# Layer norms of a gated cross-attention stack: the scaling moved from the vector engine to the scalar engine

## What is computed

```
def _layernorm(x, axis=-1, eps=1e-05):
    m = jnp.mean(x, axis=axis, keepdims=True)
    v = jnp.var(x, axis=axis, keepdims=True)
    return (x - m) / jnp.sqrt(v + eps)
...
    x = x + jnp.tanh(g_xattn[0]) * _L0_xattn_ref(_layernorm(x, axis=-1), ctx_1024, ctx_1024, L0_xattn_random_features)
    x = x + jnp.tanh(g_ffn[0]) * _L0_ffn_ref(_layernorm(x, axis=-1), ...)
...
    x = x + jnp.tanh(g_ffn[3]) * _L3_ffn_ref(_layernorm(x, axis=-1), ...)
```

## Time and profile before

| | us |
|---|---|
| median of 3 runs | 2255.64 (2252.45 to 2267.68) |
| profiled execution, its own time | 2266.98 |
| its span | 2265.2 |
| TensorE busy | 1978.6 (87%) |
| VectorE busy | 1956.1 (86%) |
| ScalarE busy | 1472.5 (65%) |
| GpSimd busy | 949.1 (42%) |

### The profile page before, as it was taken

One profiled execution on the slowest core, in us unless ns is written; L12 is line 12 of the kernel. 1 busy time (PEld: TensorE's weight loads), 2 busy tenths in 40 slices (PEclk: granted clock), 3 DMA queues, 4 the chain that ended last, 5 costly groups with the idle time before them and its releaser, 6 DMA issues. The chain is left out here.

```text
span 2265.2 us, 41466 instructions
## 1 busy us (share of the span) xinstructions
PE 1978.6 (87%) x12569; PEld 1576.8 (70%) x12569; DVE 1956.1 (86%) x7828; ACT 1472.5 (65%) x3637; POOL 949.1 (42%) x1374
## 2 busy tenths in 40 slices
PE   5877788888998899988998899998998899788677
PEld 4555567766886679766886579766886579667456
DVE  1289797998989999998989999998999999795982
ACT  3545467787677767787577767787577767477431
POOL 3232322555165534555165534555255543332441
PEclk9888898999999999999999999999999999898788
DMA  4000101001100101001100101001100001001000
GB/s 191 1 8 1 36 1 57 1 1 36 44 16 1 36 6 54 2 2 36 43 18 1 36 1 57 4 1 36 39 22 1 27 3 57 31 1 57 1 3 3
DMA packets 29503, 55.03 MB, mean 24 GB/s; under 512 B 2914, under 2 KB 10082, under 8 KB 28642
## 3 DMA queue, kind: packets, MB, share of 16 engines
q1 hardware_dynamic: 29282, 52.37, 7.1%
HBM read 51.31 MB, written 1.05 MB: 23 GB/s over the span
## 5 line engine op out<-in xcount | busy, mean ns | idle before, releaser
L265 DVE MATCH_REPLACE8 top_work<-top_eight,top_work 128x256 f32<-128x256 f32 x1664 | 667.9, 409 | 0.0
L267 DVE MAX8 top_eight<-top_work 128x8 f32<-128x256 f32 x1664 | 617.2, 412 | 0.0
L305 POOL TENSOR_TENSOR top_p<-top_p,top_rest 128x512 f32<-128x512 f32 x192 | 244.2, 1272 | 155.5 <-ACT top_rest L298 154.3
L851 PE MATMUL bank<-workP 128*128 128x256 f32 x1024 | 278.4, 396 | 22.7 <-ACT att_pP L991 10.7
L991 ACT ACTIVATE att_pP<-bank,att_tinyP 128x256 f32<-128x256 f32 x512 | 218.0, 487 | 60.4 <-DVE att_tinyP L1042 59.5
L851 PEld LDWEIGHTS bank<-workP 128*128 128x128 f32 x1024 | 180.1, 193 | 65.9 <-issue 24.2
L1042 DVE TENSOR_REDUCE att_tinyP<-bank 128x2 f32<-128x512 f32 x256 | 173.2, 680 | 22.4 <-PE bank L851 22.3
L273 POOL TENSOR_SCALAR top_nmax<-top_lead 128x2 f32<-128x2 f32 x192 | 37.2, 194 | 370.0 <-DVE top_lead L267 370.0
L645 PE MATMUL bank<-top_qk 128*128 128x256 f32 x512 | 150.0, 420 | 48.0 <-ACT top_p L286 40.7
L1013 POOL TENSOR_SCALAR workP<-workP,const 128x256 f32<-128x256 f32 x256 | 122.8, 486 | 152.8 <-PE bank L851 118.5
L298 ACT ACTIVATE top_rest<-top_work,top_nmax 128x256 f32<-128x256 f32 x384 | 173.9, 506 | 8.0 <-DVE top_work L265 7.6
(11 more groups left out here) (365 smaller groups left out, 4616.3 us busy)
## 6 DMA issues: line engine op xcount, KB each, us to landing
gelu_w<-in_pack3w SPq DMA_DIRECT2D x72, 256.0 KB, 3.0
top_qk<-in_pack3w SPq DMA_DIRECT2D x72, 256.0 KB, 2.8
pack<-in_pack SPq DMA_DIRECT2D x1, 4352.0 KB, 19.6
pack<-in_pack SPq DMA_DIRECT2D x1, 2266.0 KB, 9.7
pack<-in_pack SPq DMA_DIRECT2D x1, 1028.0 KB, 7.9
mix_wb<-in_ctx SPq DMA_DIRECT2D x1, 1024.0 KB, 4.8
x_in<-in_x SPq DMA_DIRECT2D x8, 128.0 KB, 2.1
ctx_tok<-in_ctx SPq DMA_DIRECT2D x8, 128.0 KB, 2.3
```

What stands on the lines that cost most here:

```text
L265: ins = nc.vector.match_replace(self.work[:, u % 2, j, :], eight, src, GONE)
L267: ins = nc.vector.max(eight, src)
L305: self.k.nc.gpsimd.tensor_tensor(v, v, self.rest[:, :, :], ALU.subtract).then_inc(*self.p_ready.one())
L851: mm = self.k.nc.tensor.matmul(self.banks[u % 2][:, j * T:(j + 1) * T], self.q1[:, u % self.RING, j * P:(j + 1) * P], self.kT, start=True, ...
```

## The change

VectorE no longer writes y. `dve_scale` is gone, and with it all its calls in step 1. GpSimd, after the variance, makes -mean (a new tensor_scalar), then the power as before, then their product, the bias column `shift`. ScalarE writes y = rstd * x + shift by two ACTIVATEs (Identity with a scale column and a bias column) at the place where it used to wait for the turned tile, and then waits for it and copies as before. The wait for the previous norm's transposes moves from VectorE to ScalarE. VectorE gets a wait ahead of `bn_aggr` (the previous norm's shift must be made before mean is overwritten), and GpSimd one ahead of -mean (the previous norm's y must be written before shift and rstd are overwritten), both only where a predecessor is given. The order of the steps and all other code stay as they are. The core of the diff, and one of the stages; the other stages lose their call of `dve_scale` in the same way:

```diff
@@ class LayerNorm
+        self.shift = k.sb(f"ln_shift{side}", [P, NT])
...
+        self.less, self.shift_ready = k.sem(n + "less", 1), k.sem(n + "shift", 1)
...
-    def dve_stats(self, dve):
+    def dve_stats(self, dve, before=None):
...
         self.chain.ready(dve)
+        if before is not None:
+            dve.wait_ge(*before.shift_ready.at(1))
         self.chain.mark(*(nc.vector.bn_aggr(self.mv[:, j, :], self.stats[:, j, :]) for j in range(NT)))
...
-    def dve_scale(self, dve, before=None):
+    def pool(self, pool, before=None):
+        pool.wait_ge(*self.var_ready.at(1))
         if before is not None:
-            dve.wait_ge(*before.turned.at(NT))
-        dve.wait_ge(*self.rstd_ready.at(1))
-        for j in range(NT):
-            self.k.nc.vector.tensor_scalar(self.y[:, j, :], self.x[:, j, :], self.mv[:, j, 0:1], self.rstd[:, j:j + 1],
-                                           ALU.subtract, ALU.mult).then_inc(*self.y_ready.one())
-
-    def pool(self, pool):
-        pool.wait_ge(*self.var_ready.at(1))
+            pool.wait_ge(*before.y_ready.at(NT))
+        self.k.nc.gpsimd.tensor_scalar(self.shift[:, :], self.mv[:, :, 0], -1.0, 1.0, ALU.mult, ALU.mult).then_inc(*self.less.one())
         self.k.nc.gpsimd.tensor_tensor(self.rstd[:, :], self.var[:, :], self.k.half[:, 0:NT],
                                        ALU.pow).then_inc(*self.rstd_ready.one())
+        pool.wait_ge(*self.less.at(1))
+        pool.wait_ge(*self.rstd_ready.at(1))
+        self.k.nc.gpsimd.tensor_tensor(self.shift[:, :], self.shift[:, :], self.rstd[:, :],
+                                       ALU.mult).then_inc(*self.shift_ready.one())
...
-    def act(self, act):
+    def act(self, act, before=None):
+        if before is not None:
+            act.wait_ge(*before.turned.at(NT))
+        act.wait_ge(*self.shift_ready.at(1))
+        for j in range(NT):
+            self.k.nc.scalar.activation(self.y[:, j, :], self.x[:, j, :], ACT.Identity, bias=self.shift[:, j:j + 1],
+                                        scale=self.rstd[:, j:j + 1]).then_inc(*self.y_ready.one())
         act.wait_ge(*self.turned.at(NT))
         self.k.nc.scalar.activation(self.yT[:, :], self.bank[:, 0:T], ACT.Copy).then_inc(*self.yT_ready.one())
@@ class Performer (and PlainHeads alike)
         if s == 1:
-            self.ln.act(act)
+            self.ln.act(act, self.start and self.start.ln)
...
         if s == 0:
-            self.ln.pool(pool)
+            self.ln.pool(pool, self.start and self.start.ln)
...
-            yield from self.ln.dve_stats(dve)
-        if s == 1:
-            self.ln.dve_scale(dve, self.start and self.start.ln)
+            yield from self.ln.dve_stats(dve, self.start and self.start.ln)
```

More of the change, by code:

```diff
@@ L613, in dve @@
             yield from self.ln.dve_stats(dve)
-        if s == 1:
-            self.ln.dve_scale(dve)
 class HeadsTop(TopSelect):
```

## The result

The changed kernel takes 2329.4 us (median of 4 runs, 2329.0 to 2329.5); the kernel before, on the same chip, 2255.1. The ratio is 1.032, with a 95% interval of 1.030 to 1.035: slower, by 74 us where +34 was forecast.

The account below looks back on a forecast made before the run. VectorE and TensorE, both nearly full with fixed-order queues, bound the kernel. Late y less the gain kept gave +32 us in the rolled block, norms outside +2: +34 on the median 2255.64, so 2290 us; range 2230 to 2312.

Parts of the forecast that it names:

- one clock: In the rolled block, engines were read as running at full granted clock; no term was given for a lower one.
- the 16 norms outside the rolled block: Three bare-chain norms grow by 0.8 us each, +2 us; the others, in blocks with top-k work, cost nothing.
- Removed: Sixteen writes of y per period leave VectorE: at most 8.2 us per period, 49 us over six periods.
- The pair of y: ScalarE's two ACTIVATEs per norm: 0.49 us for one, 0.87 us for the pair, bounds 0.66 to 1.10.
- rival 4: A table load around Identity, 1.28 us, two per norm: +160 us, 2420 us; chance 0.03.
- The term that decides: ScalarE writes y at the copy's place; each norm loses 1.30 us less ScalarE's earlier wait: 32 us in 1300.
- Given back: VectorE's saved time is kept only at the layer-0 heads' y, 1.01 us: 5 us in 1300.
- The added waits: VectorE's before bn_aggr and GpSimd's for the previous y look back at a norm finished several us before: nothing.
- Rivals 1 and 2: VectorE limits, others catch up: 2206 to 2231 us, chance 0.15; its waits grow by its saving: 2256 us, chance 0.20.
- Rival 3: ScalarE's earlier waiting helps nowhere and GpSimd's additions count: 53 us in 1300, 63 in the block, 2320 us; chance 0.12.

Follow-up runs that it names:

- the four other norms: The change only at the Performer, layer-0 heads, heads start and Gelu experts norms, the rest as in the kernel before: 2278.1 us, ratio 1.0082.
- the kernel with the filled wait: The changed kernel with ten idle transposes on TensorE in the wide start, between its value products and the turn of y: 2311.8 us, ratio 1.0242.
- the two kernels with 258.4 and 260.0 us periods: The change only at the Performer's and layer-0 heads' norms, 2267.5 us; and only at the gated experts' norm, 2275.5 us; the rest as in the kernel before.
- the kernel with the late four: The change only at the wide start, layer-2 heads, mix and gated experts norms, the rest as in the kernel before: 2304.0 us, ratio 1.0201.

## Why the prediction was right in sign and half the size

Three steps of the sum failed. It knew one clock, the upper one; in a steady period some 4.4 of the 10.4 us are the lower clock (an estimate, worked out below). It kept a gain of 1.0 us per period that the next hand-overs take away. And it put 2 us on the 16 norms outside the rolled block and nothing on the added waits, where the profiled spans show 9.3 us ahead of the five steady periods and 7.1 behind them, the sixth period included; the five periods themselves are 46.0 of the 62.4. The term for ScalarE's late y, which it called the deciding one, held.

**Removed.** Right: VectorE's busy time fell by 49 us (45 to 50 said), and it bought nothing, the 1.8 us per period by which y was stretched beside GpSimd's work among it.

**The pair of y.** Right. The forms L379 take 488 to 496 ns in the mean, forecast 0.49, and a pair 0.87 to 0.89, forecast 0.87:

```profile
L379 ACT ACTIVATE yP<-x,ln_shiftP,ln_rstdP 128x128 f32<-128x128 f32 x40 | 17.5, 488 | 0.0
...
L379 ACT ACTIVATE yM<-x,ln_shiftM,ln_rstdM 128x128 f32<-128x128 f32 x20 | 8.8, 496 | 0.0
```

The Trainium skill (ScalarE: Activation LUTs, What ACT_TABLE_LOAD costs) gives 186 ns and 0.833 ns per column and 93 ns for each pointer operand, 479 ns here; the trace agrees. No table load came with it, and rival 4 is out.

**The term that decides.** "What a norm loses is 1.30 less the time that ScalarE waited there before": right at M, G, S and E to 0.15 us, and by itself in the kernel with the gated norm alone (257.4 against 255.8 to 256.1, for 1.3). At H2 it was too high: where the projections ran at full clock, W>H2 grew by 0.8, not 1.3. One step of its working was loose: the rows that it quotes for the width (507 and 379 ns) differ by 128 ns and not by the 110 that it took off; the 110 fits what was measured.

**Given back.** Wrong: "I find one that is kept", 1.0 us per period. The kernel with the four other norms shows that it is lost within two experts, 0.55 us of it in a wait for ScalarE. "80 us of unbroken VectorE work" was true of the waits as they stood and not of the slack behind them: a hand-over with no wait at all may be only half a microsecond from waiting. That is 6 us over the block.

**The added waits.** Costed at nothing. The one ahead of `bn_aggr` shows 1.0 us in a period, and S>P grew by 0.18; it is back at 7.57 us in the kernel in which VectorE makes -mean. That kernel is 7 us faster by the medians with 0.2 of GpSimd's 0.5 us taken out, of which some 2 us are in the five periods, most of them with less time at the lower clock. In the blocks ahead of the first steady period the changed kernel is already 9.3 us late, and it loses 7.1 behind the last, against 2 forecast for all outside and some 5 for the rest of the block. Outside these periods ScalarE does come before the shift, as it never does in them: on side P 12 waits of 41.4 us in all, the longest 7.1 (and on side M two of 10.2),

```profile
ACT yP L379 <- POOL ln_shiftP L366: 41.4, 12, 7.1
```

of which the added 0.5 us of the chain can be 14 x 0.5 = 7 us at most, an estimate. How the 9.3 and 7.1 us divide among these norms, and how much of them is the clock, stays open; the time at 1.2 GHz outside the five periods is 197 us in the changed kernel and 189 in the one before.

**What was missing: TensorE's clock.** The sum knew one clock, since the earlier trace rows show 1.00. In the changed kernel 13.7 us of each period run at 1.2 GHz. Filling one wait of 2.27 us gives 3.5 us of the period back. What then remains, 262.7 - 255.8 = 6.9 us with 3.4 us still at the lower level, is near the 5.4 that the prediction had for a period. The distances can also be put together from periods in which each is at full clock: seven from the kernel with the filled wait and E>H0, 26.79 us, from the one with y ahead of the V copies. They make 261.8 us, 5.9 more than before (an estimate). So in a period about 6 us are the placement of y and about 4 the clock; over the whole kernel the filled wait alone is 17.6 of 74 us. The other stretches at 1.2 GHz, about the gated experts' down products and ahead of the wide start, weren't filled; that they too come from late y is argued, not shown. The kernel before has such stretches as well, in two of its five periods.

How much a lower clock costs depends on what waits for TensorE. At the projections of the wide start it was 1.67 us for eight matmuls that take 1.89, all of it on the path. Over a period it can be less: 2.5 us for 10.2 at 1.2 GHz in the two kernels with 258.4 and 260.0 us periods. The Trainium skill (TensorE: Matmul & The Clock Gate, Terms) puts the penalty at half of the time at the lower clock. By that rule 10.2 us cost 5.1; these two show a quarter rather than a half, and the measurement decides. (Between the shortest and the longest period of the kernel with the late four it is 3.3 us for 9.5, a third.) That the rest falls on matmuls that nothing waits for is likely, not shown.

**The two comparisons.** Medians say +74, the profiled spans +62. The kernel before varies from 2252 to 2268 us; its profiled execution, 11 us above the median, has 6.8 us at 1.2 GHz in each of its last two periods, and these are 257.2 and 258.4 us long, where the others are 256. The changed kernel has the lower clock in every period and varies by 0.5 us. Every execution has its mean granted clock on record, and it goes with the time: of 46 executions of the kernel before that ran beside the experiments, the six fastest (2252.3 to 2254.0 us) have 0.961 to 0.962, the four slowest (2267.6 to 2268.2) 0.953 to 0.955. So the median stands for executions with less of the lower clock than the profiled one had.

**Rivals.** Rivals 1 and 2 (VectorE the limit; it cancels) fell: the most that any hand-over caught up was the 0.5 us at H2. Rival 3 came nearest in size, 2320, but by another way: ScalarE's earlier waiting did help at G, S, P and H0, as the distances show, and GpSimd's additions counted for no more than 0.2 us of a period in the block.

## What to carry to other kernels

Work moved off the busiest engine gains nothing if its new owner does it at the point of use: ask when the new owner reaches that place, and who stands in order behind the result. Check for slack behind a gain, not for the absence of waits. And where TensorE idles a microsecond or two longer, look at the granted clock of what follows: a wait can cost its length and then more (here 3.5 us of a period behind one of 2.27), and a few idle matmuls that fill it are a cheap test (17.6 us of 74).

## What the runs showed that I had not expected

A wait of 2.27 us for one operand was followed by matmuls at 1.2 GHz in four of five steady periods in a row and in part in the fifth, one of 1.31 us at the same place (y ahead of the V copies) was not, and neither was one of 1.18 us behind ten filling transposes. But the length of the one wait doesn't decide by itself. In the kernel with the late four the same 2.27 us were followed by full clock in two of five periods; with y on VectorE behind the shift, 1.29 us at this place were followed by the lower clock in four of five; and the kernel before has waits of TensorE of 3.0, 2.5 and 2.5 us elsewhere in its periods and runs three of the five at full clock throughout.

The same kernel can settle into periods of different length in one execution: 255.9 and 258.4, 257.4 and 260.0, 261.9 and 265.2 us, and each time the longer has more time at 1.2 GHz. In the last pair one matmul group, 1.89 or 3.56 us, makes half of the step; in the other two that group takes 1.89 in every period, and the step lies between the gated experts and the wide start.

Busy time misleads: VectorE's MAX8 records (L267 from top_work) have a mean of 430 ns after and 412 before, but its rounds start 1.44 us apart in both kernels. TensorE's busy time rose by 30 us for the same matmuls. Neither is more work.
